# A decoder layer on one core: another order of steps in the five engine tables

## What is computed

```python
x = x + attn(layernorm(x), Wq, Wk, Wv, Wo)                  # stage a, 8 heads
x = x + xattn(layernorm(x), ctx, fside + fside + SxS2_mask, # stage b, 16 heads
              Wq, bq, Wk, bk, Wv, bv, Wo, bo)
x = x + sum_e w_e * (relu(ln(x) @ w1_e.T)**2 @ w2_e.T) \
      + relu(ln(x) @ cfc.T)**2 @ cproj.T                    # stage c, 8 experts + shared
```

## Time and profile before

| what | us |
|---|---|
| median of 3 runs | 2286.68 (2283.66 to 2294.39) |
| the profiled execution | 2293.97 |
| span of its trace, first to last instruction | 2292.2 |
| busy PE / ACT / DVE / POOL | 2090.7 / 2025.3 / 1861.8 / 1780.7 |

### The profile page before, as it was taken

How to read it: one execution, slowest core, us unless ns; L and a number is a source line. 1 busy time by engine, 2 the same in 40 slices (tenths; PEclk the granted TensorE clock), 3 DMA queues, 4 the chain that set the end, 5 groups by cost and what they waited for, 6 DMA issues and landing times.

```text
span 2292.2 us, 72843 instructions
## 1 busy us (share of the span) xinstructions
PE 2090.7 (91%) x24128; PEld 1813.5 (79%) x24128; DVE 1861.8 (81%) x6768; ACT 2025.3 (88%) x5937; POOL 1780.7 (78%) x1899
## 2 busy tenths in 40 slices
...
GB/s 131 132 197 175 164 173 175 171 169 195 172 166 167 178 169 171 202 170 168 166 174 167 177 186 165 174 174 180 156 192 181 166 171 174 181 160 189 167 136 18
DMA packets 650854, 383.91 MB, mean 167 GB/s; under 512 B 557808, under 2 KB 590832, under 8 KB 650480
## 3 DMA queue, kind: packets, MB, share of 16 engines
...
...
## 4 chain that ended last, share of the span: by engine, by line
PE 54%; issue 12%; POOL 10%; ACT 8%; DMA 6%; DVE 5%; SPq 4%; ACTq 0%; DVEq 0%; POOLq 0%
PE ps_c_hidden L974 14%; PE ps_c_out L974 13%; PE ps_a_misc L974 12%; DMA b_probsT_hi_lo<-b_probs_hi_lo 5%; PE ps_b_misc L1111 4%; SPq L394 3%; PE ps_b_scores L1097 3%; POOL bias L518 3%; PE ps_a_misc L1053 2%; ACT c_relu L680 2%; ACT ps_b_probs L654 2%; ACT a_qT_hi L599 2%; POOL ctxT_hi L484 1%; ACT ps_b_probs L652 1%; PE ps_a_misc L1054 1%
## 5 line engine op out<-in xcount | busy, mean ns | idle before, releaser
L518 POOL TENSOR_TENSOR bias<-bias,b_mask 128x512 f32<-128x512 f32 x512 | 645.1, 1274 | 6.6 <-DMA bias<-in_bias 6.3
L834 DVE CUSTOM_DVE_ANT_0 b_neg_scores<-ps_b_scores,bias 128x256 f32<-128x256 f32 x1024 | 391.4, 419 | 69.6 <-POOL bias L518 35.6
L841 DVE TENSOR_TENSOR b_probs_hi_lo<-ps_b_probs,b_probs_hi_lo 128x512 f16<-128x512 f32 x512 | 352.0, 687 | 105.9 <-ACT b_probs_hi_lo L662 103.5
L539 POOL TENSOR_TENSOR c_hidden_lo<-c_hidden,c_hidden_hi 128x512 f16<-128x512 f32 x288 | 335.2, 1164 | 49.1 <-issue 33.4
L974 PE MATMUL ps_c_hidden<-c_xT_hi,w_hi 128*128 128x256 f16 x1152 | 316.7, 275 | 20.4 <-ACT c_relu L680 20.4
L974 PE MATMUL ps_c_out<-w_hi,c_hidden_hi 128*128 128x256 f16 x1152 | 318.9, 277 | 8.9 <-DVE acc L945 8.9
L532 POOL TENSOR_TENSOR c_hidden<-c_relu 128x512 f32<-128x512 f32 x288 | 299.8, 1041 | 31.9 <-ACT c_relu L680 12.5
L974 PE MATMUL ps_c_out<-w_lo,c_hidden_hi 128*128 128x256 f16 x1152 | 319.1, 277 | 0.0
L974 PE MATMUL ps_c_out<-w_hi,c_hidden_lo 128*128 128x256 f16 x1152 | 318.9, 277 | 0.0
L974 PE MATMUL ps_c_hidden<-c_xT_lo,w_hi 128*128 128x256 f16 x1152 | 316.2, 274 | 0.0
L974 PE MATMUL ps_c_hidden<-c_xT_hi,w_lo 128*128 128x256 f16 x1152 | 316.2, 274 | 0.0
...
## 6 DMA issues: line engine op xcount, KB each, us to landing
bias<-in_bias SPq DMA_DIRECT2D x256, 512.0 KB, 4.1
qk_scratch<-b_qT_hi_lo SPq DMA_DIRECT2D x128, 128.0 KB, 3.2
qk_scratch<-b_kT_hi_lo SPq DMA_DIRECT2D x128, 128.0 KB, 2.6
...
```

The source lines that it names most:

```text
L518: gp.tensor_tensor(part, part, b_mask[:, :], ALU.add).then_inc(b_c_ok, 1)
L539: gp.tensor_tensor(c_hl[:, u, :], c_h[:, :], c_hh[:, u, :], ALU.subtract).then_inc(c_h_ok, 1)
L834: last = dve.tensor_tensor_reduce(out=b_t[:, u, c, :], in0=ps_bs[:, c * T:(c + 1) * T], in1=bias[:, slot, at:at + T], scale=-2.0, scalar=3 ...
L841: dve.tensor_tensor(b_p2[:, j % DEPTH, :, 1, :], ps_bp[:, :].rearrange("p (c t) -> p c t", c=CT), b_p2[:, j % DEPTH, :, 0, :], ALU.subtrac ...
```

## The change

Only the five tables and LAGS change; each table holds the same entries as before. Of the tables for SP and POOL all is shown, of the others the lines that matter here.

```diff
@@ -74,53 +74,53 @@
 
 ORDERS = {name: order(text) for name, text in dict(
     sync="""
-        b_store_q:0@4 b_pT:15@5 b_store_k:0@4 b_stack_q:0@4 b_stack_k:0@4 b_pT:0@4 c_f2:8@6 b_pT:1@4 b_load:0@4
-        b_mask:0@4 b_load:1@4 b_pT:2@4 a_ln:0@3 b_pT:3@4 b_load:2@4 b_pT:4@4 b_pT:5@4 b_pT:6@4 b_load:3@4
-        b_pT:7@4 b_pT:8@4 b_pT:9@4 b_load:4@4 b_load:5@4 b_pT:10@4 b_pT:11@4 b_load:6@4 a_T:0@2 w_load:4@2
-        w_load:5@2 w_load:6@2 w_load:7@2 w_load:8@2 w_load:9@2 w_load:10@2 w_load:11@2 w_load:12@2 w_load:13@2
-        w_load:14@2 w_load:15@2 w_load:16@2 w_load:17@2 w_load:18@2 w_load:19@2 b_pT:12@4 b_pT:13@4 b_pT:14@4
-        b_load:7@4 b_split_q:0@3""",
+        w_load:11@5 b_pT:7@6 b_pT:8@6 w_load:12@5 w_load:13@5 b_pT:9@6 b_pT:10@6 b_load:4@6 b_load:5@6
+        w_load:14@5 b_pT:11@6 w_load:15@5 b_pT:12@6 b_load:6@6 w_load:16@5 b_pT:13@6 b_load:7@6 a_T:0@4
+        b_pT:14@6 b_pT:15@6 w_load:17@5 b_split_q:0@5 w_load:18@5 b_store_q:0@5 b_store_k:0@5 b_stack_q:0@5
+        b_stack_k:0@5 w_load:19@5 w_load:4@4 c_f2:8@7 w_load:5@4 w_load:6@4 w_load:7@4 b_load:0@5 b_pT:0@5
+        b_pT:1@5 b_pT:2@5 b_load:1@5 b_pT:3@5 b_mask:0@5 b_load:2@5 w_load:8@4 w_load:9@4 b_pT:4@5 b_pT:5@5
+        b_pT:6@5 b_load:3@5 w_load:10@4 a_ln:0@4""",
     gpsimd="""
-        c_f1:1@6 c_lo:1@6 b_res:0@5 c_f1:2@6 c_lo:2@6 b_comb:6@5 c_f1:3@6 b_comb:7@5 c_lo:3@6 c_f1:4@6
-        b_comb:8@5 b_comb:9@5 c_lo:4@6 c_f1:5@6 b_comb:10@5 b_comb:11@5 c_lo:5@6 b_comb:12@5 a_ln:0@3
-        b_comb:13@5 b_comb:14@5 c_f1:6@6 c_lo:6@6 c_f1:7@6 b_comb:15@5 b_ln:0@4 c_lo:7@6 a_kv:0@3 a_q:0@3
-        b_comb:0@4 b_split_q:0@4 a_q:1@3 c_f1:8@6 b_split_k:0@4 a_q:2@3 b_comb:1@4 c_lo:8@6 a_q:3@3 b_comb:2@4
-        c_ln:0@5 b_kv:0@3 b_comb:3@4 b_comb:4@4 b_comb:5@4 b_v:0@4 c_f1:0@5 c_lo:0@5""",
+        c_lo:2@6 c_f1:3@6 c_lo:3@6 a_ln:0@3 c_f1:4@6 b_res:0@5 b_comb:9@5 b_comb:10@5 c_lo:4@6 b_comb:11@5
+        b_comb:12@5 c_f1:5@6 b_comb:13@5 b_kv:0@4 c_lo:5@6 c_f1:6@6 c_lo:6@6 b_comb:14@5 b_ln:0@4 b_comb:15@5
+        a_kv:0@3 a_q:0@3 c_f1:7@6 c_lo:7@6 b_split_q:0@4 a_q:1@3 c_f1:8@6 b_split_k:0@4 a_q:2@3 c_lo:8@6 a_q:3@3
+        b_comb:0@4 b_comb:1@4 b_comb:2@4 c_ln:0@5 b_comb:3@4 b_comb:4@4 b_comb:5@4 b_comb:6@4 b_comb:7@4
+        c_f1:0@5 b_v:0@4 c_lo:0@5 c_f1:1@5 c_lo:1@5 b_comb:8@4 c_f1:2@5""",
     scalar="""
...
-        b_s:6@2 a_pv:5@1 b_p:6@2 c_f1:6@3 a_n:7@1 b_s:7@2 c_sq:5@3 w_split:12@1 b_p:7@2 a_pt:7@1 a_pv:6@1
-        w_split:13@1 b_s:8@2 b_p:8@2 w_split:14@1 w_split:15@1 a_pv:7@1 c_f1:7@3 w_split:3@0 b_s:9@2 b_p:9@2
-        c_sq:6@3 b_s:10@2 b_p:10@2 a_ln:0@0 b_s:11@2 b_p:11@2 a_T:0@0 c_f1:8@3 w_split:4@0 b_s:12@2 w_split:5@0
-        b_p:12@2 a_kv:0@0 c_sq:7@3 b_s:13@2 b_ln:0@1 b_p:13@2 w_split:6@0 b_T:0@1 a_q:0@0 b_s:14@2 b_p:14@2
-        a_q:1@0 b_q:0@1 b_s:15@2 b_p:15@2 a_s:0@0 b_kv:0@1 a_n:0@0 c_sq:8@3 a_s:1@0 a_q:2@0 a_pt:0@0 a_n:1@0
-        a_s:2@0 a_pt:1@0 a_pv:0@0 a_q:3@0 b_o:0@2 a_s:3@0 a_s:4@0 a_n:2@0 a_n:3@0 a_pv:1@0 a_pt:2@0 a_s:5@0
-        a_n:4@0 w_split:7@0 a_s:6@0 c_ln:0@2 a_pt:3@0 a_n:5@0 c_T:0@2 b_v:0@1 b_s:0@1 a_pv:2@0 b_p:0@1 a_n:6@0
-        a_pt:4@0 w_split:8@0 c_gate:0@2 c_f1:0@2 b_s:1@1 c_sq:0@2 b_p:1@1 c_f1:1@2 a_pv:3@0""",
...
+        c_sq:8@4 a_n:1@1 a_s:2@1 a_q:3@1 a_pt:1@1 a_n:2@1 b_o:0@3 a_s:3@1 a_pv:0@1 a_s:4@1 a_n:3@1 a_pt:2@1
+        a_s:5@1 a_pv:1@1 a_n:4@1 a_s:6@1 c_ln:0@3 a_pt:3@1 a_n:5@1 c_T:0@3 b_s:0@2 a_pv:2@1 w_split:7@1 b_p:0@2
+        a_pt:4@1 c_gate:0@3 b_v:0@2 c_f1:0@3 b_s:1@2 c_sq:0@3 b_p:1@2 c_f1:1@3 a_n:6@1 b_s:2@2 c_sq:1@3 b_p:2@2
...
+        c_sq:4@3 b_s:7@2 c_f1:6@3 w_split:9@1 b_p:7@2 a_pv:6@1 a_pt:7@1 b_s:8@2 b_p:8@2 a_pv:7@1 w_split:10@1
+        a_ln:0@0 c_sq:5@3 b_s:9@2 b_p:9@2 c_f1:7@3 b_s:10@2 w_split:11@1 b_p:10@2 c_sq:6@3 b_s:11@2 w_split:12@1
+        b_p:11@2 a_T:0@0 w_split:13@1 c_f1:8@3 w_split:14@1 b_s:12@2 w_split:15@1 b_p:12@2 w_split:3@0 a_kv:0@0
+        b_ln:0@1 b_s:13@2 b_p:13@2 w_split:4@0 b_T:0@1 a_q:0@0 w_split:5@0 c_sq:7@3 b_s:14@2 w_split:6@0
...
     vector="""
...
-        c_f2:2@4 a_pv:5@2 b_p:6@3 b_s:8@3 c_f2:3@4 b_s:9@3 w_split:12@2 b_p:7@3 a_pt:7@2 a_pv:6@2 w_split:13@2
-        w_split:14@2 b_s:10@3 w_split:15@2 a_pv:7@2 b_p:8@3 a_ln:0@1 a_ln:1@1 c_f2:4@4 b_p:9@3 b_s:11@3 b_p:10@3
...
-        b_mask:0@2 a_q:0@1 b_s:14@3 b_p:13@3 b_T:0@2 a_q:1@1 b_s:15@3 b_p:14@3 b_q:0@2 a_s:0@1 b_r:0@3 b_p:15@3
...
+        c_f2:3@4 b_s:9@3 b_p:7@3 a_pv:6@2 a_pt:7@2 b_s:10@3 w_split:9@2 a_pv:7@2 w_split:10@2 b_p:8@3
+        w_split:11@2 b_p:9@3 c_f2:4@4 w_split:12@2 b_s:11@3 b_p:10@3 a_wo:0@2 b_s:12@3 b_ln:0@2 b_p:11@3 a_T:0@1
+        b_ln:1@2 b_s:13@3 c_f2:5@4 b_p:12@3 w_split:13@2 a_kv:0@1 b_s:14@3 b_mask:0@2 a_q:0@1 b_p:13@3 b_T:0@2
...
     tensor="""
-        a_kv:0@2 b_pv:7@4 c_f2:6@5 a_q:0@2 b_pv:8@4 b_s:14@4 b_pv:9@4 b_T:0@3 a_q:1@2 b_s:15@4 b_pv:10@4 b_q:0@3
...
-        a_pt:1@2 b_pv:14@4 b_pv:15@4 a_pv:0@2 a_s:4@2 b_o:0@4 c_f2:8@5 a_s:5@2 b_wo:0@4 a_pv:1@2 a_pt:2@2
-        a_s:6@2 b_kv:1@3 a_s:7@2 a_pt:3@2 a_pv:2@2 c_T:0@4 b_s:0@3 a_pt:4@2 b_s:1@3 c_gate:0@4 c_f1:0@4 b_s:2@3
-        a_pv:3@2 c_f1:1@4 a_pt:5@2 b_s:3@3 c_f1:2@4 c_f2:0@4 b_s:4@3 c_f1:3@4 a_pv:4@2 c_f2:1@4 b_s:5@3 c_f1:4@4
-        a_pt:6@2 c_f2:2@4 b_s:6@3 c_f1:5@4 b_pv:0@3 b_s:7@3 b_pv:1@3 a_pv:5@2 c_f1:6@4 b_s:8@3 b_pv:2@3 c_f2:3@4
-        a_pv:6@2 a_pt:7@2 b_s:9@3 c_f1:7@4 c_f2:4@4 b_s:10@3 a_pv:7@2 b_pv:3@3 b_pv:4@3 b_pv:5@3 b_s:11@3
...
+        a_pv:7@3 c_f2:4@5 b_s:11@4 a_wo:0@3 b_s:12@4 c_f1:8@5 a_T:0@2 b_pv:7@4 b_s:13@4 c_f2:5@5 a_kv:0@2
+        b_s:14@4 b_pv:8@4 c_f2:6@5 a_q:0@2 b_T:0@3 b_pv:9@4 b_pv:10@4 b_s:15@4 a_q:1@2 b_q:0@3 a_s:0@2 a_q:2@2
...
+        b_pv:15@4 a_pt:1@2 a_pv:0@2 a_s:4@2 b_o:0@4 c_f2:8@5 a_s:5@2 b_wo:0@4 a_pt:2@2 a_s:6@2 a_pv:1@2 b_kv:1@3
+        a_pt:3@2 b_s:0@3 c_T:0@4 b_s:1@3 a_pv:2@2 a_pt:4@2 c_gate:0@4 c_f1:0@4 a_s:7@2 b_s:2@3 c_f1:1@4 a_pv:3@2
+        b_s:3@3 a_pt:5@2 c_f1:2@4 b_pv:0@3 c_f2:0@4 b_s:4@3 c_f1:3@4 c_f2:1@4 b_s:5@3 a_pv:4@2 c_f1:4@4 c_f2:2@4
...
+        a_pt:7@2 b_pv:3@3 b_pv:4@3 c_f1:7@4 b_s:10@3 b_pv:5@3 b_pv:6@3""",
 ).items()}
-LAGS = 6
+LAGS = 7
 
 
 def after(batch, per_batch, n):
...
```

More of the change, by code:

```diff
@@ L113 @@
-    tensor="""
-        a_kv:0@2 b_pv:7@4 c_f2:6@5 a_q:0@2 b_pv:8@4 b_s:14@4 b_pv:9@4 b_T:0@3 a_q:1@2 b_s:15@4 b_pv:10@4 b_q:0@3
-        a_s:0@2 a_q:2@2 b_pv:11@4 b_kv:0@3 a_s:1@2 b_pv:12@4 c_f2:7@5 b_pv:13@4 a_s:2@2 a_pt:0@2 a_q:3@2 a_s:3@2
-        a_pt:1@2 b_pv:14@4 b_pv:15@4 a_pv:0@2 a_s:4@2 b_o:0@4 c_f2:8@5 a_s:5@2 b_wo:0@4 a_pv:1@2 a_pt:2@2
-        a_s:6@2 b_kv:1@3 a_s:7@2 a_pt:3@2 a_pv:2@2 c_T:0@4 b_s:0@3 a_pt:4@2 b_s:1@3 c_gate:0@4 c_f1:0@4 b_s:2@3
-        a_pv:3@2 c_f1:1@4 a_pt:5@2 b_s:3@3 c_f1:2@4 c_f2:0@4 b_s:4@3 c_f1:3@4 a_pv:4@2 c_f2:1@4 b_s:5@3 c_f1:4@4
-        a_pt:6@2 c_f2:2@4 b_s:6@3 c_f1:5@4 b_pv:0@3 b_s:7@3 b_pv:1@3 a_pv:5@2 c_f1:6@4 b_s:8@3 b_pv:2@3 c_f2:3@4
-        a_pv:6@2 a_pt:7@2 b_s:9@3 c_f1:7@4 c_f2:4@4 b_s:10@3 a_pv:7@2 b_pv:3@3 b_pv:4@3 b_pv:5@3 b_s:11@3
-        a_wo:0@2 c_f1:8@4 b_s:12@3 a_T:0@1 b_pv:6@3 c_f2:5@4 b_s:13@3""",
+        w_load:11@5 b_pT:7@6 b_pT:8@6 w_load:12@5 w_load:13@5 b_pT:9@6 b_pT:10@6 b_load:4@6 b_load:5@6
```

28 lines of the change are left out of this document (17 added, 11 removed).

## The result

The changed kernel takes 2259.03 us in the median of 4 runs (2255.84 to 2271.02); the kernel before, with its run beside it, 2285.17. Between the two profiled executions it is 37.3 us (2293.97 to 2256.65).

A forecast was written before the change was run, and what follows sets the result against it. No engine was full, so the order of work was taken to bound the kernel. Sum: 31 x (1.5 + 0.69) = 67.9, plus 6.5 at the start: 2293.97 - 74.4 = 2220 us; range 2182 to 2273.

The forecast's parts named there:

- a_n:6: On ACT, moved from ahead of c_f1:0 to behind c_f1:1: shortens ACT's gapless part by 0.69 us a batch, lower bound 0.
- the first term: On SP, b_pT:15 issued before the context load and q's stores: 1.5 us a batch, bounds 1.18 and 2.04.
- b_pT:15 ahead of the stores: On SP, issued 3.7 us earlier, removing PE's wait for head 15's transposed probabilities: 1.5 us a batch.
- The other swaps ... whose sum stays: 0: On PE, b_s:0, a_s:7, c_f2:4 and b_pv:0 reordered: steps of 0.3 to 1.3 us inside its gapless part, gain 0.
- rival B: The stack loop, with 3.2 us slack before b_s:0, limits the cycle to 65.3 us: 2235 us, chance 0.14.
- POOL's split at 0: On POOL, context split from behind c_ln to ahead of c_lo:5: 0, bound 0.5 either way.
- Start and tail: Start: weight pieces moved behind ACT's a_kv and a_pv:7 save 6.5 us, bounds 0 and 10; tail left at 135.7.
- wrong if the cycle stays above 66.3: Sign against the forecast: a cycle staying above 66.3 us, where 64.8 was forecast.
- Rival C: On DVE, b_mask lengthened by 0.96 us in every batch, uncovered: 30 us on the forecast, 2250 us, chance 0.04.
- Rival D: SP's later residual load delays DVE's a_wo: 2273 us, near no change, chance 0.08; or 2328, slower, chance 0.09.

The follow-up runs named there:

- e4: Kernel before with one SP entry moved: b_pT:15 ahead of the context load and the four stores of q; 2241.39 us, ratio 0.9786 to before.
- e2: Changed kernel with the next context's load on SP moved from ahead of the stores of q to behind the stack loads; 2235.51 us, ratio 0.9751 to before.
- e13: Changed kernel with eight idle matmuls on PE ahead of b_s:0's wait for the stacks; 2245.22 us, ratio 0.9802 to before.
- e11: e2 with ACT's a_n:6 put back in its old place behind b_p:0; 2242.20 us, ratio 0.9787 to the kernel before.
- e10: e4 with the context load on SP moved behind the stack loads; 2252.92 us, ratio 0.9834 to the kernel before.
- e15: e10 with POOL's context split moved from behind c_ln to ahead of c_lo:5; 2257.38 us, ratio 0.9859 to the kernel before.
- e5: Kernel before with only the weight pieces (w_load, w_split) at the places of the changed kernel; 2291.94 us, ratio 1.0000 to before.

## Why the prediction was wrong

The forecast had 2.19 us a batch, and 0.66 came. Of the 1.53 missing, 0.69 are a_n:6, 0.11 the first term's excess over what e4 gives alone, and 0.73 (66.31 against e4's 65.58) what the rest of the change takes away again, where the forecast had 0.

- **b_pT:15 ahead of the stores: right.** 1.5 us a batch was forecast; e4 gives 1.39 in the mean cycle (66.97 to 65.58). Part of this is luck: at full clock it is 1.09 (66.81 to 65.72), near PE's own wait of 1.18, and the rest is that the falls behind the old wait end, which had no term.
- **"The other swaps ... whose sum stays: 0" failed.** PE's part was added up as if only its own length counted. The swaps bring b_s:0 2.1 us forward against stacks that come no earlier, the stores of q even later (15.8 us behind a_wo before, 17.95 after), and PE waits 1.31 us a batch there. e2 and e13, which work on this wait alone, give 21 and 11 us back, so it is a cause of the 0.73; how much of the 0.73 each swap makes stays open, since no run that put PE's steps back was faster. The slack of 3.2 us was there in rival B, which I gave 0.14 and priced at 65.3 a batch, and its sign came, a wait at L1097 behind the landing of k_stack_odd. The cycles at full clock last 65.55 with 0.88 us of this wait; that they would be 0.88 shorter without it isn't shown, and e2 speaks against it.
- **The clock had no term.** The trace of before held 5 cycles of 69.3 us against 66.8, which I had averaged away. After, 13 cycles are 2.11 us longer than the rest, 27 us, where before 5 were 2.49 longer, 12 us: the difference is 15 of the 47 us that the cycles fell short by. It contains the longer waits of these cycles, and overlaps the 0.73 above.
- **a_n:6's 0.69 failed too.** It came in no run. On e4 the move lengthens the cast by 0.23 us and the cycle by 0.26; in the new order its sign is open (e11). PE waits only 0.56 us a batch (11.7/21) for relus in the kernel before, at most 0.3 at a time, so no more than that could reach PE by the relus.
- **b_pv:6** (now ahead of a_wo) is most of PE's 9.3/21 = 0.44 us a batch of waits for transposed probabilities, 7.8 of the 9.3 us. It was costed at nothing among the swaps.
- **POOL's split at 0:** on e10 it took POOL's wait for the context away and gained nothing (e15); alone on the kernel before it was not run.
- **Start and tail** were undersized: 11.9 for 6.5, 4.9 for 0. The reason given for the start was wrong: the weight pieces alone gain no time (e5). How much of the tail is the clock isn't separated.
- **Rival C** named a mechanism that these traces show, at the wrong instruction: b_mask's L820 keeps its median (417 to 419 ns), while casts of L903 go from 0.50 us to 1.03 in about half of the batches and to 0.16 in the others. What that costs is open. **Rival D** didn't come about; L740 waits for no DMA.
- The range, 2182 to 2273, holds 2259.03, but only by its upper end, which stood for rival D. The time lies there for another reason, and that is luck. The sign "wrong if the cycle stays above 66.3" came, if only just: 66.31.

What stays open: why e2's order still has PE wait up to 3.3 us for the stacks in single cycles, which moves make the start's gain, and what each of PE's swaps costs by itself.
